# A graph layer whose adjacency is transposed on TensorE: one of four chunks is turned by VectorE from a second, block-wise load

## What is computed

```python
h = relu(layernorm(x))
HW = einsum('bnf,rfo->rbno', h, W[:, :F]) + (W_edges @ W[:, F:])[:, None, None, :]   # 7 relations
A_list = [A, A, shifted, A^T, A^T, shifted^T, eye]
out = max over r of (A_list[r] @ HW[r]) + bias
x = x + out
```

## Time and profile before

| | |
|---|---|
| Median of 3 runs | 221.91 us (221.73 to 223.33) |
| The profiled execution, own time | 223.7 us |
| Its span (first to last instruction) | 221.7 us |
| Share of the span in which an engine is busy | PE 95%, ACT 84%, DVE 81%, POOL 74% |
| DMA, main queue, share of 16 engines' span | 70.3% |
| Granted TensorE clock | 0.994 of full speed on average |

### The profile page before, as it was taken

One profiled execution on the slowest core, in us unless ns is written; L12 is line 12 of the kernel. 1 busy time (PEld: TensorE's weight loads), 2 busy tenths in 40 slices (PEclk: granted clock), 3 DMA queues, 4 the chain that ended last, 5 costly groups with the idle time before them and its releaser, 6 DMA issues.

```text
span 221.7 us, 4960 instructions
## 1 busy us (share of the span) xinstructions
PE 211.5 (95%) x1069; PEld 174.5 (79%) x1069; DVE 179.2 (81%) x388; ACT 186.0 (84%) x468; POOL 163.8 (74%) x179
## 2 busy tenths in 40 slices
PE   7898999999999999999999999999999999999980
PEld 5777678887888888888888888888888888887760
DVE  3795799796989879797887969887887969777683
ACT  3767999998998989898898989899898989887640
POOL 1370499979596996969697896969699696969241
PEclk9999999999999999999999999999999999999997
DMA  5928976959596986768596877758597776236725
GB/s 178 302 91 184 243 199 171 263 113 252 135 248 143 245 180 157 231 158 215 122 254 145 198 206 155 235 136 218 131 230 190 165 222 146 43 53 143 158 37 89
DMA packets 91152, 38.71 MB, mean 175 GB/s; under 512 B 71575, under 2 KB 80903, under 8 KB 91143
## 3 DMA queue, kind: packets, MB, share of 16 engines
q1 hardware_dynamic: 90055, 38.48, 70.3%
q10 hardware_dynamic: 1088, 0.13, 0.4%
HBM read 34.33 MB, written 4.26 MB: 174 GB/s over the span
## 4 chain that ended last, share of the span: by engine, by line
PE 85%; DVE 6%; ACT 2%; DMA 2%; issue 2%; SPq 0%; DVEq 0%; ACTq 0%
PE at_ps L745 11%; PE rel_ps L765 11%; PE rel_ps L767 11%; PE rel_ps L766 11%; PE bwd_ps L765 6%; PE bwd_ps L767 6%; PE bwd_ps L766 6%; PE fwd_ps L765 6%; PE fwd_ps L767 6%; PE fwd_ps L766 6%; PE turn_ps L753 3%; DMA a_sb<-in_adj 2%; DVE h_lo L692 1%; DVE best L595 1%; PE rel_ps L762 1%
## 5 line engine op out<-in xcount | busy, mean ns | idle before, releaser
L304 POOL TENSOR_TENSOR a_lo<-a_sb,a_hi 128x512 fp32r<-128x512 f32 x62 | 79.1, 1298 | 37.8 <-ACT a_hi L386 37.8
L595 DVE TENSOR_TENSOR best<-rel_ps,best 128x512 f32<-128x512 f32 x62 | 42.6, 687 | 13.7 <-PE rel_ps L767 13.6
L566 DVE TENSOR_TENSOR at_lo<-at_ps,at_hi 128x512 fp32r<-128x512 f32 x62 | 41.2, 685 | 8.2 <-ACT at_hi L394 7.6
L434 ACT ACTIVATE rel_ps<-sum_all,c_col 128x512 f32<-128x512 f32 (+1 forms) x63 | 41.8, 679 | 4.5 <-DVE best L595 2.9
L386 ACT ACTIVATE a_hi<-a_sb 128x512 fp32r<-128x512 f32 x64 | 39.4, 617 | 3.8 <-DMA a_sb<-in_adj 3.8
L394 ACT ACTIVATE at_hi<-at_ps 128x512 fp32r<-128x512 f32 x62 | 36.3, 590 | 6.5 <-PE at_ps L745 6.3
L745 PEld LDWEIGHTS at_ps<-ident,a_sb 128*128 128x128 f32 x240 | 28.1, 141 | 4.2
L745 PE MATMUL at_ps<-ident,a_sb 128*128 128x128 f32 x240 | 31.2, 272 | 0.0
L592 DVE SCALAR_TENSOR_TENSOR best<-rel_ps,c_col,best 128x512 f32<-128x512 f32 x32 | 23.9, 747 | 6.9 <-PE rel_ps L767 5.8
L319 POOL TENSOR_TENSOR xb_sb<-xp_sb,bias_sb 128x512 f32<-128x512 f32 x16 | 22.7, 1421 | 5.9 <-DMA xp_sb<-in_x 5.9
L765 PE MATMUL bwd_ps<-a_hi,h_hi 128*128 128x512 f32 x64 | 27.0, 421 | 0.0
(11 more groups left out here) (103 smaller groups left out, 438.9 us busy)
## 6 DMA issues: line engine op xcount, KB each, us to landing
a_sb<-in_adj SPq DMA_DIRECT2D x64, 256.0 KB, 3.3
sum_all<-sums_dram SPq DMA_DIRECT2D x16, 512.0 KB, 4.1
x_sb<-in_x SPq DMA_DIRECT2D x16, 256.0 KB, 3.7
xp_sb<-in_x SPq DMA_DIRECT2D x64, 64.0 KB, 3.6
out<-o_sb SPq DMA_DIRECT2D x60, 64.0 KB, 2.0
w_sb<-in_L_gnn_W SPq DMA_DIRECT2D x1, 448.0 KB, 6.0
sums_dram<-sum_rows SPq DMA_DIRECT2D x16, 4.0 KB
bias_sb<-in_L_gnn_b SPq DMA_DIRECT2D x4, 64.0 KB, 2.2
```

What stands on the lines that cost most here:

```text
L304: pool.tensor_tensor(a_lo[q][:, j, :], a_sb[q][:, j, :], a_hi[q][:, j, :].bitcast(fp32), ALU.subtract).then_inc(a_lo_ready[j], 1)
L434: act.activation(to[:, cols], sum_all[q][:, 0 if r in FWD else 1, cols], ACT.Copy, scale=c_col[:, r:r + 1]).then_inc(after_it, 1)
L566: dve.tensor_tensor(at_lo[q][:, i, :], at_bank(b, i)[:], at_hi[q][:, i, :].bitcast(fp32), ALU.subtract).then_inc(at_lo_ready[i], 1)
L595: dve.tensor_tensor(best[q][:], held[:], best[q][:], ALU.max).then_inc(joined[r], 1)
```

## The change

Chunk 3 of the transposed adjacency of batches 1 to 15 is no longer made by TensorE. SyncE loads the 128 columns of A that it comes from a second time, from DRAM, by blocks into `a_blocks` (four transfers of 64 KB); VectorE turns it in 32x32 blocks into `at_last` (`turn_a_blocks`), in SBUF; ScalarE and VectorE then read `at_last` where they read the PSUM bank before. Both tensors have a single buffer. Batch 0 keeps the old way. `reload_a` issues two transfers of 512 KB in place of four of 256 KB and waits for the GpSimd halves in pairs.

```diff
         def at_from(b, i):
+            if i == C - 1 and not is_batch(b, 0):
+                return at_last
             return rel_ps[i] if isinstance(b, int) and b == 0 and i < 2 else at_ps[i % 2]
...
             def reload_a(k, q):
-                sp.wait_ge(a_turned[C - 1], b + 1)
-                for j in range(C):
-                    sp.wait_ge(a_lo_ready[j], b + 1)
-                    load_a(k + 1, q, j)
+                sp.wait_ge(a_turned[C - 2], b + 1)
+                if is_batch(b, 0):
+                    sp.wait_ge(first_turned, 1)
+                for first in range(0, C, 2):
+                    sp.wait_ge(a_lo_ready[first], b + 1)
+                    sp.wait_ge(a_lo_ready[first + 1], b + 1)
+                    sp.dma_start(a_sb[q][:, first:first + 2, :],
+                                 adj[2 * k + 2 + q, first * P:(first + 2) * P, :].rearrange("(j p) m -> p j m", p=P)
+                                 ).then_inc(a_loaded[q][first + 1], 16)
+
+            def load_a_blocks(k, q):
+                b = 2 * k + q
+                wait(sp, a_turned[C - 1], b - 1)
+                load_by_blocks(a_blocks, adj[b, :, (C - 1) * P:], a_blocks_loaded)
...
                 load_xp(k, q)
+                if more:
+                    load_a_blocks(k + 1, q)
...
             for j in range(C):
                 load_a(0, 1, j)
+            load_a_blocks(0, 1)
...
+            def turn_a_blocks(k, q):
+                b = 2 * k + q
+                dve.wait_ge(a_blocks_loaded, G * 16 * b)
+                if not is_batch(b, 1):
+                    dve.wait_ge(at_lo_ready[C - 1], b)
+                dve.transpose(at_last[:], a_blocks[:]).then_inc(a_turned[C - 1], 1)
...
                     round_h(*ahead)
+                    turn_a_blocks(*ahead)
                 join(*prev, FWD[1])
...
                 if left:
                     turn_a(*ahead, 2)
-                    turn_a(*ahead, 3)
```

More of the change, by code:

```diff
@@ L72, in gnn_layer @@
         a_lo = pair(sb, "a_lo", [P, C, N], fp32r)
+        a_blocks = sb("a_blocks", [P, N])
+        at_last = sb("at_last", [P, N])
         at_hi = pair(sb, "at_hi", [P, C, N], fp32r)
@@ L108, in gnn_layer, with is_batch, at_from @@
         sums_dram = [nc.dram_tensor(f"sums_dram{q}", [S, P], fp32, kind="Internal").ap() for q in range(2)]
-        def at_bank(b, i):
+        def is_batch(b, n):
+            return isinstance(b, int) and b == n
+        def at_from(b, i):
+            if i == C - 1 and not is_batch(b, 0):
+                return at_last
             return rel_ps[i] if isinstance(b, int) and b == 0 and i < 2 else at_ps[i % 2]
@@ L117, in gnn_layer @@
         x_loaded, xp_loaded = pair(sem, "x_loaded"), sem("xp_loaded")
+        a_blocks_loaded, first_turned = sem("a_blocks_loaded"), sem("first_turned")
         out_stored = pair(sem, "out_stored")
@@ L162, in before @@
             return (k, 0) if q == 1 else (k - 1, 1)
-        def is_batch(b, n):
-            return isinstance(b, int) and b == n
         def rel_bank(b, r):
@@ L382, in round_a @@
                 b = 2 * k + q
-                act.wait_ge(a_loaded[q][j], 16 * (k + 1))
+                act.wait_ge(a_loaded[q][j if isinstance(k, int) and k == 0 else j // 2 * 2 + 1], 16 * (k + 1))
                 wait(act, bwd_done, b - 1)
@@ L390, in round_at @@
                 b = 2 * k + q
-                act.wait_ge(a_turned[i], b + 1)
+                if is_batch(b, 0) and i == C - 1:
+                    act.wait_ge(first_turned, 1)
+                else:
+                    act.wait_ge(a_turned[i], b if i == C - 1 else b + 1)
                 wait(act, fwd_done, b - 1)
                 wait(act, sums_turned, b - 1)
-                act.activation(at_hi[q][:, i, :], at_bank(b, i)[:], ACT.Copy,
+                act.activation(at_hi[q][:, i, :], at_from(b, i)[:], ACT.Copy,
                                accum_out=sums[q][:, 1, i:i + 1]).then_inc(at_hi_ready[i], 1)
@@ L565, in split_at @@
                 wait(dve, fwd_done, b - 1)
-                dve.tensor_tensor(at_lo[q][:, i, :], at_bank(b, i)[:], at_hi[q][:, i, :].bitcast(fp32),
+                dve.tensor_tensor(at_lo[q][:, i, :], at_from(b, i)[:], at_hi[q][:, i, :].bitcast(fp32),
                                   ALU.subtract).then_inc(at_lo_ready[i], 1)
@@ L736, in turn_a @@
                 if i == 0:
-                    for j in range(C):
+                    for j in range(C) if isinstance(k, int) and k == 0 else (1, 3):
                         pe.wait_ge(a_loaded[q][j], 16 * (k + 1))
-                if i >= 2:
-                    pe.wait_ge(at_lo_ready[i - 2], b + 1)
+                if i == 2:
+                    pe.wait_ge(at_lo_ready[0], b + 1)
+                elif i == 0:
+                    pe.wait_ge(at_lo_ready[2], b)
                 else:
-                    pe.wait_ge(at_lo_ready[i + 2], b)
+                    pe.wait_ge(at_lo_ready[C - 1 if is_batch(b, 1) else 1], b)
                 for j in range(C):
-                    last = pe.transpose(at_bank(b, i)[:, j * P:(j + 1) * P], a_sb[q][:, j, i * P:(i + 1) * P], ident[:])
+                    last = pe.transpose(at_from(b, i)[:, j * P:(j + 1) * P], a_sb[q][:, j, i * P:(i + 1) * P], ident[:])
                 last.then_inc(a_turned[i], 1)
@@ L898, in _ @@
                 for i in range(C):
-                    last = pe.transpose(at_bank(0, i)[:, j * P:(j + 1) * P], a_sb[0][:, j, i * P:(i + 1) * P], ident[:])
+                    last = pe.transpose(at_from(0, i)[:, j * P:(j + 1) * P], a_sb[0][:, j, i * P:(i + 1) * P], ident[:])
                     if j == C - 1:
-                        last.then_inc(a_turned[i], 1)
+                        last.then_inc(first_turned if i == C - 1 else a_turned[i], 1)
             first_step()
```

## The result

The changed kernel takes 237.6 us (median of 4 runs, 237.05 to 240.64) against 222.6 for the kernel before: ratio 1.068, 95% interval 1.062 to 1.074. It is slower by 15 us; the forecast was 217.5.

The account below looks back on a forecast made before the run. TensorE, busy throughout the middle steps, was taken as the bound: 6.1 us saved, less 1.4 at the start and 0.3 at the end, is 4.4 us, so 221.91 - 4.4 = 217.5 us; range 215.2 to 222.0.

Parts of the forecast that it names:

- The bound now, and the work on TensorE: Middle steps: TensorE bounds; dropping a chunk of transposes saves 0.435 us in 14 steps, 6.1 us, giving steps of 12.26 us.
- Cost on the path: 0: VectorE's new turn after the rounding of h delays later work by 0.2 to 0.6 us, but TensorE does not wait.
- The prediction's own bounds: Whole kernel: 215.8 us with start and end free, 218.8 with upper costs, 1.4 more for leaks; given as 215.3 to 219.7.
- VectorE, ScalarE, the wait for `a_blocks`: Each step: VectorE's 0.70 us turn and ScalarE's 0.03 us more fit into 12.26 us; `a_blocks` lands with 0.8 us slack.
- The rival: `split_at` 3 on VectorE, now with two SBUF operands, waits 1.29 us for GpSimd each step; 222.4 us, chance 0.09.
- SyncE: the step that failed: SyncE's queue: four more issues, 1.93 us, covered by its own waiting; cost 0, or 0.7 us a step if 3.96 us.
- The sums come late by part of the gain: Rival at the fill: longer landing times make `sum_all` or the blocks late; 220.6 us, or 222 to 223; chance 0.11.
- DMA as the bound: Slower rival: small runs cost twice as much, a step holds 13.2 us of DMA and waits; 228.9 us, chance 0.10.
- The DMA time itself: Second load each step: 1.65 us of all 16 DMA engines, from 9.9 to 11.6 us of 12.26, share 0.94.

Follow-up runs that it names:

- 4: Changed kernel with the block-wise load made once, for batch 1, and those columns turned again for every later batch: 221.1 us, ratio 0.989.
- 10: Kernel of 8 with VectorE's new turn moved behind the maximum with relation 1: 222.3 us, ratio 1.000.
- 13: As 4, the changed kernel with the block-wise load made once, and VectorE's turn behind the maximum with relation 1: 219.9 us, ratio 0.986.
- 8: Changed kernel with SyncE storing the sums first, then the output, and only then waiting for the sums and issuing `sum_all`: 222.2 us, ratio 0.993.
- 7: Changed kernel with the store of the turned sums issued by ScalarE in place of SyncE: 227.2 us, ratio 1.013.
- 14: Kernel before with four issues more per step, each of 4 KB in 32 runs, which nothing reads: 239.7 us, ratio 1.073.
- 5: Changed kernel whose second load takes the last 128 rows in 2 KB runs, in place of 128 columns in 128-byte runs: 237.2 us, ratio 1.062.
- 6: Changed kernel with the second load's four issues each cut from 64 KB to 4 KB from batch 2 on: 237.1 us, ratio 1.057.
- 15: Changed kernel with two small issues per step for the second load in place of four: 225.1 us, ratio 1.010.

## Why the prediction was wrong

**The bound now, and the work on TensorE: right, with a size.** TensorE bounded the step, and with the load out of the way (4) the step shortened. The term was 14 x 0.435 = 6.1 us; measured 12 steps x 0.27 = 3.2 us. Half of the steps reach 12.27 to 12.30 us, against 12.26 forecast, so the saving itself was sized right; longer steps between them bring the mean to 12.45. The prediction put the turn's place in VectorE's order at "Cost on the path: 0"; behind the maximum (10, 13) the short steps are more frequent. In the two long steps looked at there, ScalarE waits for `sum_all`; what makes all the others long stays open. Up to the first mark 4 loses 0.8 us (43.34 against 42.58), and behind the last it gains 0.4 (26.1 us to the end of the span, against 26.5). 3.2 - 0.8 + 0.4 = 2.8 us is the difference of the spans, 221.7 and 218.9. The changed kernel has much the same ends, 0.9 lost and 0.5 gained, so its loss lies in the steps.

The prediction's own bounds do not add up either: 218.8 + 1.4 is 220.2, not 219.7, and the lower one, 215.8, became 215.3. The measured time is far outside both.

**VectorE, ScalarE, the wait for `a_blocks`: right but for the turn's place.** They fit; the turn took 704 ns and waited 0.2 us in all for its load. The two SBUF operands of `split_at` 3 did not collide. Its neighbour did: the rounding of h, 749 ns before on average, took 1047 ns in 4 and 1235 in 8, where it falls beside GpSimd's `o_sb`. The rival had the mechanism at the wrong instruction, and it did not make the loss: in the changed kernel that rounding averages 713 ns.

**SyncE: the step that failed.** The text said: "1.93 is covered ... I take 0 in the middle, with 0.7 a step as the other end." It cost 14.11 - 12.45 = 1.7 us a step. The cover was counted right, 3.2 us of SyncE's waiting for GpSimd, and the four issues were nearly sized right (2.4 to 2.9 us). Wrong was that the cover can be spent while all else stays as it is. The spacing of the transfers came from those waits. Without them SyncE issues the reloads of x and the adjacency back to back, 1.3 MB, and the four stores and the 4 KB of the sums right behind; these issues then stall (2.81 and 2.36 us in place of 1.98 and 0.39), the round trip waits longer (1.78 in place of 1.21), and, in the step shown, the sum is the step: 0.35 + 1.93 + 2.42 + 0.39 + 1.00 + 2.81 + 2.36 of issue, 1.78 of landing and some 1.2 of small gaps are 14.2 us. With the stores, the sums and the wait at 1.98, 0.39 and 1.21 us, as before, the same sum is 10.9 us and would fit: the four issues do not fill the queue by themselves, the 3.4 us of stalls that come with them do. That SyncE's serial order is the bound is shown: by 8, which takes the round trip out of it and brings the step back to 12.56 us (43.42 to 194.19) with the same transfers; by 7; and by 14. That the stalls come from the crowding of the transfers ahead of the stores is argued from the order of the rows; no run took the crowding alone away. Why the queue does not settle back into the spaced pattern, for which it would have 1.4 us to spare, is open too.

**The sums come late by part of the gain: the right symptom.** The prediction's third rival named `sum_all` late at the fill, through longer landing times, at 0.11. It was late through its issue, by up to 3 us and not 1 (ScalarE waited 20.9 us in 11 times, 1.9 on average); its landing time did not grow. That rival was cut off at the loss of the gain; a serial queue that has become the bound has no such floor.

**DMA as the bound: wrong mechanism on the right side.** It was the slower rival, at 0.10 and 228.9 us. The DMA time itself was forecast well: 0.72 of 151.92 us, twelve steps of the kernel before (47.38 to 199.30), are 9.1 us a step, and 0.77 of 141.92 us, ten steps of the changed kernel (49.05 to 190.97), are 10.9 us: 1.8 us more, against 1.65 priced. But it was not what bound. Little of the loss is its: with long runs (5) the ratio is 1.062 and with a sixteenth of the bytes (6) 1.057, against 1.068.

**A rule of the Trainium skill.** The runs moved one 4 KB issue from SyncE to ScalarE and gained 10 us (7). The Trainium skill, "DMA: Bandwidth & Descriptors" (Issuing engines are not separate DMA queues), says that issuing from several engines at once only saves the sequencer's time to initiate a transfer, which is usually small relative to the transfer. The first half agrees; the second does not here: a 4 KB issue held the sequencer for 2.36 us at 116.08, longer than the 1.78 us for which SyncE then waited for it, and the queue's issues and its one wait summed to the length of the step.

## What to carry to other kernels

An issuing queue is an engine with a busy time of its own: add up its issues and its waits for landings per step, and compare the sum with the step, before pricing bytes. Leave a margin: here the sum at the old prices was 10.9 us of some 12.3, and the prices rose. Waiting time on it is cover only until it is used up, and it also keeps transfers apart; near that point two issues cost 4 us and four cost 16 (15 and 6 against 4). A wait for a round trip in such a queue is the place to put other issues.

## What the hardware showed that was not expected

- The cost of a transfer to its issuer followed what stood before it more than what it carried: four issues of 64 KB took 2.42 us, four of 4 KB 2.66 us (14), and one of 4 KB 0.30 us after an idle stretch (8, 107.59) and 2.36 us behind a full one (116.08).
- The kernel was 16.5 us slower at a DMA share of 0.68 (14) and level at 0.93 (8), each in a window of one step: here the share told nothing of a queue's limit.
- A rounding from SBUF to SBUF on VectorE took 1.30 us in 8, from 105.80, and 0.61 us in the kernel before, from 105.04. Beside both ran GpSimd's `o_sb`; this is the row of the kernel before:

```profile
104.07 1.29 POOL L326 TENSOR_TENSOR o_sb<-turned,xb_sb 128x512 f32<-128x512 f32 x1
```

GpSimd ends at 105.36 and the rounding at 105.65; in 8 they end at 106.81 and 107.10. Both times the rounding ends 0.29 us after GpSimd's instruction, so its length was set by how late in that instruction it began. The contention was there before the change.
